# Local layers of a Trainium2 megakernel: the feed-forward normalisation is moved half a slot later, its rows are turned at the slot's end, two gate products open the next slot

## The reference, cut to what matters

```
for i in range(DEPTH):                                   # DEPTH = 6
    x = attn_layer(shift_tokens(x), ...) + x             # 16 heads of 64, windows of 32, look back one window
    x = ffn_layer(shift_tokens(x), ...) + x

def ffn_layer(x, g, bln, W1, b1, W2, b2):
    mu  = x.mean(-1, keepdims=True)
    var = ((x - mu) ** 2).mean(-1, keepdims=True)
    xn  = (x - mu) / jnp.sqrt(var + 1e-05) * g + bln
    hg  = xn @ W1 + b1
    a, gate = jnp.split(hg, 2, -1)                       # 341 columns each
    return a * jax.nn.gelu(gate, approximate=False) @ W2 + b2
```

## Time and profile before

| | |
|---|---|
| runs | 2888.02 us median; 2883.43, 2896.18 |
| profiled execution, first to last instruction | 2885.9 us |
| PE busy | 2561.9 us, 89% |
| POOL busy | 1823.8 us, 63% |
| DVE busy | 1733.7 us, 60% |
| ACT busy | 1463.1 us, 51% |
| granted clock of PE, mean | 0.907 |

### The profile page before, as it was taken

How to read it: one execution, slowest core, us unless ns; L and a number is a source line. 1 busy time by engine, 2 the same in 40 slices (tenths; PEclk the granted TensorE clock), 3 DMA queues, 4 the chain that set the end, 5 groups by cost and what they waited for, 6 DMA issues and landing times. The chain is left out here.

```text
span 2885.9 us, 97353 instructions
## 1 busy us (share of the span) xinstructions
PE 2561.9 (89%) x40447; PEld 1739.3 (60%) x40447; DVE 1733.7 (60%) x3455; ACT 1463.1 (51%) x2654; POOL 1823.8 (63%) x3086
## 2 busy tenths in 40 slices
PE   6848999986989999999999999999999999599976
PEld 1227888873656666666666666666666666345544
DVE  6822222224767777777777767777777776466624
ACT  5722222212666666666666666665666666235532
POOL 0045666524988888888888888888788886113321
PEclk9968889856999999999999999999999999779977
DMA  1001111103211212221222122122211111000000
GB/s 33 0 23 37 38 38 38 38 23 116 55 41 43 60 46 71 55 61 46 72 55 61 46 63 60 43 60 63 63 46 44 46 44 47 26 2 4 4 2 15
DMA packets 113247, 124.87 MB, mean 43 GB/s; under 512 B 40990, under 2 KB 71342, under 8 KB 112046
## 3 DMA queue, kind: packets, MB, share of 16 engines
q1 hardware_dynamic: 112814, 118.69, 14.9%
HBM read 35.80 MB, written 8.91 MB: 15 GB/s over the span
## 5 line engine op out<-in xcount | busy, mean ns | idle before, releaser
L1730 POOL TENSOR_TENSOR l_rot_a<-l_rot_a,l_rot_b 128x512 f32<-128x512 f32 x384 | 483.0, 1273 | 105.6 <-DVE l_rot_b L1590 105.3
L1584 DVE TENSOR_TENSOR l_rot_a<-l_A,l_tab 128x512 f32<-128x512 f32 x384 | 264.9, 690 | 279.9 <-ACT l_sq L1452 257.1
L1220 PE MATMUL l_A<-l_wts,l_H 128*128 128x512 f32 x768 | 418.4, 629 | 13.9 <-DMA l_maskb<-in_l_mask 10.1
L1739 POOL TENSOR_TENSOR l_qk<-l_rot_a,l_rn 128x512 f32<-128x512 f32 x384 | 388.3, 1042 | 21.8 <-POOLq L1777 21.8
L1452 ACT ACTIVATE l_sq<-l_A 128x512 f32<-128x512 f32 x384 | 231.0, 602 | 144.2 <-PE l_A L1220 139.7
L1458 ACT ACTIVATE l_pT<-l_T 128x512 f32<-128x512 f32 x192 | 108.9, 595 | 374.2 <-PE l_T L1266 373.8
L1590 DVE TENSOR_TENSOR l_rot_b<-l_A,l_tab 128x512 f32<-128x512 f32 x384 | 261.3, 681 | 0.0
L1594 DVE TENSOR_REDUCE l_ss<-l_sq 128x8 f32<-128x512 f32 x384 | 259.6, 676 | 0.0
L1321 PE MATMUL l_T<-ident,l_qk 128*128 128x128 f32 x1536 | 212.0, 281 | 22.1 <-POOL l_qk L1739 16.6
L1321 PEld LDWEIGHTS l_T<-ident,l_qk 128*128 128x128 f32 x1536 | 176.2, 143 | 87.0 <-issue 58.2
L1802 POOL TENSOR_TENSOR l_pn<-l_sd,l_rs 128x1024 f32<-128x1024 f32 x96 | 182.7, 1903 | 68.6 <-DVE l_rs L1612 68.6
(11 more groups left out here) (340 smaller groups left out, 5627.4 us busy)
## 6 DMA issues: line engine op xcount, KB each, us to landing
l_vw<-l_vn SPq DMA_DIRECT2D x384, 128.0 KB
l_vw<-l_vn SPq DMA_DIRECT2D x360, 64.0 KB
l_wts<-in_l_wts SPq DMA_DIRECT2D x18, 650.0 KB, 5.1
c_lower_out<-c_amt SPq DMA_DIRECT2D x16, 384.0 KB, 2.5
c_inv<-c_first_in SPq DMA_DIRECT2D x16, 384.0 KB, 3.3
l_tab<-in_l_tables SPq DMA_DIRECT2D x6, 1024.0 KB, 5.1
l_wts<-in_l_wts SPq DMA_DIRECT2D x6, 635.5 KB, 4.9
result<-x SPq DMA_DIRECT2D x4, 256.0 KB, 2.3
```

Source lines behind the costliest of these rows:

```text
L1220: pe.matmul(A[j % 2][:], cols(m), w_of(m)[:, C_QKV + 512 * j:C_QKV + 512 * j + 512], start=True, stop=True).then_inc(pq_done, 1)
L1584: dve.tensor_tensor(rot_a[p][:, j, :].rearrange("p (a d) -> p a d", d=DH), src.rearrange("p (a d) -> p a d", d=DH), table[:, a, t:t + 1, : ...
L1730: pool.tensor_tensor(rot_a[m % 2][:, j, :], rot_a[m % 2][:, j, :], rot_b[:, j, :], ALU.add).then_inc(rot_rdy, 1)
L1739: pool.tensor_tensor(qk[:, j, :].rearrange("p (a d) -> p a d", d=DH), rot_a[p][:, j, :].rearrange("p (a d) -> p a d", d=DH), rn[p][:, 8 * ...
```

## The change

Nothing is added or taken away: the same instructions run in another order. The normalisation (both halves) moves from the end of the slot of offset 1 to the middle of the slot of offset 2: on DVE behind `soft_shift`, on ACT behind `keep_outputs`. `turn_norm` and `keep_norm` move from the middle to the end of the slot of offset 2, where the first two gate products and their gelus were. These open the slot of offset 3, on PE ahead of `project(n+2, 1)`, `masks`, and gate product 2, on ACT ahead of `square(n+2, 1)` and the third gelu. On DVE product 0 now follows `rope(n+2, 1)`. The wait of `values` for xnT goes.

```diff
@@ PE, values: @@
-                if group_at(n, 2) is not None:
-                    pe.wait_ge(xnT_rdy, group_at(n, 2) + 1)
@@ PE, turn_norm: @@
                 pe.wait_ge(xn_rdy, k + 1)
-                pe.wait_ge(v_rdy, 2 * min(n, TILES - 1) + 1)
-                pe.wait_ge(oS_rdy, 2 * min(n - 1, TILES))
+                bank_free(n, 0)
@@ PE, slot: @@
                 if group_at(n, 3) is not None:
                     k = group_at(n, 3)
+                    pe.wait_ge(xnT_rdy, k + 1)
+                    for i in range(2):
+                        bank_free(n - 1, i)
+                        gates(k, i)
+                if has(n + 2):
+                    project(n + 2, 1)
+                if has(n):
+                    masks(n)
+                if group_at(n, 3) is not None:
+                    k = group_at(n, 3)
                     pe.wait_ge(gl_rdy, 3 * k + 1)
                     gates(k, 2)
                     pe.wait_ge(gl_rdy, 3 * k + 2)
                     linears(k, 0)
-                if has(n + 2):
-                    project(n + 2, 1)
-                if has(n):
-                    masks(n)
...
                     scores(n, range(HP))
-                if group_at(n, 2) is not None:
-                    turn_norm(n, group_at(n, 2))
...
                 if group_at(n, 2) is not None:
-                    k = group_at(n, 2)
-                    pe.wait_ge(xnT_rdy, k + 1)
-                    for i in range(2):
-                        bank_free(n, i)
-                        gates(k, i)
+                    turn_norm(n, group_at(n, 2))
@@ ACT, slot: @@
                 if group_at(n, 3) is not None:
-                    gelu(group_at(n, 3), 2)
+                    for i in range(2):
+                        gelu(group_at(n, 3), i)
                 if has(n + 2):
                     square(n + 2, 1)
-                if group_at(n, 2) is not None:
-                    k = group_at(n, 2)
-                    if k % 4 == 0:
-                        act.wait_ge(w_ld[(k // 4) % 2], w_need(k // 4))
-                    keep_norm(k)
+                if group_at(n, 3) is not None:
+                    gelu(group_at(n, 3), 2)
...
                     keep_outputs(n - 1)
+                if group_at(n, 2) is not None:
+                    normed(n, group_at(n, 2))
...
                 if group_at(n, 2) is not None:
-                    for i in range(2):
-                        gelu(group_at(n, 2), i)
+                    k = group_at(n, 2)
+                    if k % 4 == 0:
+                        act.wait_ge(w_ld[(k // 4) % 2], w_need(k // 4))
+                    keep_norm(k)
...
                     keep_oT(n - 1)
-                if group_at(n, 1) is not None:
-                    normed(n, group_at(n, 1))
@@ DVE, slot: @@
+                if has(n + 2):
+                    rope(n + 2, 1)
                 if group_at(n, 3) is not None:
                     product(group_at(n, 3), 0)
-                if has(n + 2):
-                    rope(n + 2, 1)
...
                     soft_shift(n)
+                if group_at(n, 2) is not None:
+                    normed(n, group_at(n, 2))
...
                     rope(n + 2, 3)
-                if group_at(n, 1) is not None:
-                    normed(n, group_at(n, 1))
```

More of the change, by code:

```diff
@@ L1516, in normed @@
                     c = 2 * HEADS + i
-                    last = act.activation(xn[:, i, :], xt[:, i, :], ACT.Identity, scale=rn[n % 2][:, c:c + 1], bias=shift[:, i:i + 1])
+                    last = act.activation(xn[:, i, :], xt[:, i, :], ACT.Identity, scale=rn[(n - 1) % 2][:, c:c + 1], bias=shift[:, i:i + 1])
                 last.then_inc(xn_rdy, 1)
@@ L1640, in normed @@
             def normed(n, k):
-                r = rn[n % 2][:, 2 * HEADS:]
-                dve.wait_ge(rn_rdy, n + 3 if has(n + 2) else TILES + k - GROUPS + 3)
+                r = rn[(n - 1) % 2][:, 2 * HEADS:]
+                dve.wait_ge(rn_rdy, n + 2 if has(n + 1) else TILES + k - GROUPS + 3)
                 dve.scalar_tensor_tensor(shift[:], mv[:, :, 0], -1.0, r, ALU.mult, ALU.mult).then_inc(shift_rdy, 1)
```

## The result

The changed kernel takes 2796.85 us (median of 4; 2783.97 to 2798.91) against 2891.4 us for the kernel before in the same comparison: ratio 0.9672, 95% interval 0.9635 to 0.9710. The forecast was 2780 us, with a range of 2745 to 2838. Two later comparisons of the same kernel gave 0.9654 (0.9614 to 0.9694) and 0.9664 (0.9624 to 0.9703).

A forecast was written before the change was run, and what follows sets the result against it. PE was taken to bound the period (72.85 us), with a hole in one slot of four. Over 22 groups 51.6 + 39.6 + 45 - 29 = 107 us go, from 2885.9 to about 2779; forecast 2780, range 2745 to 2838.

The forecast's parts named there:

- The hole and its cause: Slot of offset 2: PE idle 3.87 us, clock 0.86, because DVE waits for the roots with the next slot's rotation queued.
- PE's wait for xn, 51.6 us: PE's wait before `turn_norm` in the slot of offset 2 goes, 51.6 us; 8.1 us in the drain stay.
- PE's wait for h, 39.6 us: PE's wait before the second half of `turn_probs`, offset 2, goes: 22 x 1.80 = 39.6 us of 42.8.
- The clock, 45 us: PE's lower clock in the slot of offset 2 goes: 2.05 us a group, 45 us over 22; bounds 0 and 53.
- New stalls, 29 us: PE stalls of 0.1 + 0.6 + 0.1 + 0.5 = 1.3 us a group come with the new order, 29 us.
- the 0.6 and 0.5 us of PE: PE stalls a group: 0.6 us at `turn_norm` until O0's value copy, 0.5 at gate 2 until gelu 0 frees O0.
- Rival A: The clock still falls behind PE's new stalls, so 45 us stay: 2825 us, chance 0.20.
- B: ACT's table load before the gelus brings the skill rule's drain of about 1380 ns: 31 us less gain, 2811, chance 0.05.
- C: POOL becomes the bound, q and k late in the slot of offset 2: about 33 us, 2813, chance 0.10.
- D: Slower: the PE-ACT chain from `turn_norm` to gate 2 at the head of offset 3 is exposed; 36 us, 2924, chance 0.05.
- E: No change: 3.9 us idle and the low clock reappear at the new place; 2888, chance 0.05.

The follow-up runs named there:

- the filled idle time: The kernel before with extra matmuls, their result unused, in PE's two idle stretches of the slot of offset 2: 2871.35 us, ratio 0.9925.
- the added work: The changed kernel plus eight small dependent POOL instructions behind `probs`: 2795.17 us in the slot of offset 2, 2815.41 us in that of offset 1.

## Why the prediction was right, point by point

- *The hole and its cause.* Right. DVE's wait for the roots, with `add_back` queued behind it, was the head of the chain; DVE's half put back alone loses all.
- *PE's wait for xn, 51.6 us.* Right: all of it is gone from the 22 slots. The drain took 2.9 more, so the total fell by 59.7 - 11.0 = 48.7.
- *PE's wait for h, 39.6 us.* Too much: these waits add up to 33.4 us in the 22 slots. The term took 1.80 us for each group from one row, and the earlier trace rows said that 1.8 is the longest.
- *The clock, 45 us.* Somewhat too much. PE's busy time in the 22 slots fell by 36.3 us, 1.65 a slot in place of 2.05. The term was worked out from the slot at 2080.33, whose busy time fell by 2.4 (20.49 to 18.11); the mean slot lost less. With the waits left in place the clock alone is worth 25 us, as the filled idle time showed.
- *New stalls, 29 us.* Too much: PE's idle time in the 22 slots is 86.1 before, of which the two waits were 85.0, and 19.7 after, so 18.6 came. Of the 19.7, 4.8 are the wait for vn and 1.4 one for qk; 10.8 are idle time with no wait ("issue", 1.1 before), which no term had. The stalls themselves were over-priced because I put ACT's instructions end to end, and most start about 0.1 us before the one ahead ends, so after ten of them xnT came at t = 10.2 and not 10.8, and the first gelu at 13.1 and not 13.5; the 0.6 and 0.5 us of PE shrank to at most 0.3 at L1350 and nearly nothing at the third gate.
- The errors are opposite: with the measured terms the sum is 51.6 + 33.4 + 36.3 - 18.6 = 102.7, forecast 107. The waits and the clock were 15 us too high, the new stalls 10; that the sum came so close is partly luck.
- *The rest of the miss* (2797 against 2780) is mostly the stage ahead: 11 us of it in the profiled execution, and nothing in the prediction spoke of it.
- *Rival A* did not come: the clock is 0.99 over 830 to 2420 us, and 1.00 over 830 to 2330, where it was 0.96 before. *B*: the gelu again starts 0.02 us after the load ends (2023.01 + 1.28, 2024.31). By the rule of the Trainium skill (ScalarE: Activation LUTs, What ACT_TABLE_LOAD costs) there would be a drain of about 1380 ns, and no trace here has one. *C*: true of the direction only, as the added work showed. *D, E*: no; but `keep_norm` 1.7 us later gives the wait for xnT that D feared.

## What to carry to other kernels

Where an in-order engine waits long, read what stands behind the waiting instruction on that engine, not only who waits for its result: the instruction of 0.16 us, put back, cost over 110 us (local layers of 1738.1 us against 1623.8) through the additions and the maximum queued behind it. Move such an instruction behind the urgent work of its own engine, to a place where its input has long been made, and check with added work how long the cover is, that is, how much later the result could come before anyone waits. When costing a hole, take the mean over all groups, of the waits and of the engine's busy time, and not one row's or one slot's; and don't charge idle time and a lower clock for the same microsecond.

## What the runs showed of the hardware that was not expected

PE also idles with no wait, inside long rows of small matmuls ("issue", 21.5 us at L1293 above). In the change's first trace the one slot of the steady part with a fall of the clock lies behind the longest of these; the gap, then the slot that it lies in:

```profile
1117.86 0.25 PE L1293 MATMUL l_O<-l_vw,l_pT 64*32 64x64 f32 x3 [2.10 <-issue]
```
```profile
1112.84:1134.78 21.94, 19.84 (x331) 12.89 (x332) 13.14 (x20) 14.88 (x26) 19.85 (x34) 0.92 0.32 95
```

The gap is not enough for a fall, though. The change's repetition has one as long in the same place, with the clock at 1.00:

```profile
1098.76 0.25 PE L1293 MATMUL l_O<-l_vw,l_pT 64*32 64x64 f32 x3 [2.12 <-issue]
```
```profile
1093.71:1114.78 21.07, 18.57 (x332) 12.10 (x332) 12.62 (x20) 14.59 (x26) 18.89 (x34) 1.00 0.34 98
```

The DMA shares of 0.32 and 0.34 stand beside 0.17 in the slot at 2011.25. Whether the instructions came late because of that traffic was not tried.
